# Second half of a fused vision tower: Gram products as one block, half-array routed sums, and the next rows turned ahead of the first pair's values

## The chip, the cores and the metric

The kernel runs on one core of one Trainium2 chip. The metric is the device time of one execution, in microseconds. A core has TensorE (PE in the profile; matrix products and transposes into PSUM), VectorE (DVE), ScalarE (ACT), GpSimd (POOL) and SyncE (SP, which issues the DMAs). Each engine works through its own queue in order and waits on semaphores for the others.

## What is computed

64 images of 64 patches each, 256 features, two layers of attention and feed-forward. In short:

```python
h  = patches(x) @ tokW + b                       # 64 images x 64 rows x 256
h += top-k sparse attention(layernorm(h))        # 16 heads
h += shared FFN(layernorm(h)); the routed experts' rows (2 of 8, grouped by counts)
h += polymax attention(layernorm(h)) @ W_proj
# polymax(s) = (s*s + 1 if s > 0, 1 - 0.01*s if -100 <= s <= 0, else 0) / 1000, causal
g  = gelu(rmsnorm(layernorm(h)) @ sign(w_up)-like ternary.T)
h += (g / (rms(g) + 1e-8)) @ ternary(w_down).T
```

The rms of g over its 1024 features is needed only as a factor of each output row, so the kernel multiplies first and scales afterwards.

## The kernel before

The images are taken in 8 slots of 8 images, 512 rows, four tiles of 128 rows. The first half runs the first layer's attention and shared FFN over the slots; the second half (from about 425 us) runs the second layer, slot after slot, in `slot_B(g, prev, nxt, routed)`, written out once for every engine. Slot 0 has no slot before it, slots 1 to 4 are a hardware loop (`Fori(1, LAST - 2)`, with `routed="batch"`), slot 5 is `"last"`, slot 6 has nothing routed, slot 7 has no next slot. PSUM has eight banks of 128 x 512 f32.

In slot g TensorE does, in this order: scores of tiles 2 and 3 of g; the rest of the Gram products of slot g-1; `B2_values(g, 0)`; `B3_down(g-1)` for tiles 0 and 1; the first projection; `B3_down(g-1)` for tiles 2 and 3; transposes of the next slot's normed rows `xn1` (two chunks, banks 4 and 5); `routed_sums` and `routed_turn`; `B1_qk(g+1)`; `B2_values(g, 1)`; the second projection; `routed_gates` or `routed_out`; `B1_v(g+1)`; transposes of `xn2`; scores of tiles 0 and 1 of g+1; and `B3_up(g)`.

- `B3_up` (L677) makes the eight up products (1024 hidden features, 128 at a time) into three banks. ScalarE turns each into a Gelu (L971), makes a 16-bit high half (L961), VectorE makes the low half (L1612, `g_parts`, semaphore `gl_out`).
- `gram` (L689) makes, per slice f of 128 hidden features, 16 small products whose diagonals add up to the sum of squares of each row of g. Slices 0 to 3 stand among the up products (`GRAM_LAG = 4`), slices 4 to 7 in the next slot. VectorE reads the diagonals in `mean_squares` (L1619), POOL takes the root, VectorE the reciprocal (`one_over_rms`).
- The scores become polymax weights in this way: ScalarE makes the relu (`relus`, L947) and the linear part (`lins`, L952), the square is made by VectorE for tiles 0, 1 (`v_quads`, L1562) and by ScalarE for 2, 3 (L957), VectorE adds and masks in `poly` (L1550, L1556).
- `stats3`, POOL's power (L1041) and `norm3` (L1168) norm the next slot's rows; TensorE turns them (L326); ScalarE and VectorE make 16-bit halves (L920, L1540) for `B1_qk` (L336) and `B1_v` (L621).
- `turned` (L1566) brings the values' output to SBUF for the projection (L664); `projected` (L1573) adds it to the rows; `stats4`, POOL (L1074) and `norm4` norm them for the up products; `ffn_out` (L1634) adds the FFN's output of slot g-1.
- The routed rows come in four batches of 16 groups (RB = 16). VectorE makes `one_hots` (L1477), TensorE turns them (L571) and takes gate rows from a small table (L581), VectorE weights them (`gates_in`, L1498), ScalarE and VectorE apply silu (L915, L1505), VectorE makes `weighted_hots` (L1511), and in the next slot `routed_sums` (L560) sums the batch: `wz` (128 columns) stands in the array and 64 columns of the one-hots move. In the first slot it sums zeroed buffers. `sums_in` adds the 128 x 64 result to `racc`.

Of the kernel before, what the change touches and what calls it, by code (L numbers as in the profile page):

```python
# [54 lines left out]
def build(nc, x, tokW, tokb, wqkv, bqk, bv, rW1, rb1, rW2, rb2, gateW, eb, w1, w3, w2, s1, s3, s2,  # L55
          wat, wpr, wup, wdn, ident, par, sel, delta, rev64, cmask, ridx, iota64, rev8, out):
    with ExitStack() as ctx:
# [93 lines left out]
        racc = sb("racc", [P, 64]); gT = sb("gT", [P, 64])  # L151
        UP_BANKS = (4, 7, 5)
        GRAM_LAG = 4
# [62 lines left out]
        gl_out, gT_ok, h1_mm, h1_out, h2_ok, quadv_ok = sems("gl_out gT_ok h1_mm h1_out h2_ok quadv_ok")  # L216
        h3_ok, h4_ok, h5_ok, high_w, hs_ok, hs_split, k_mm = sems("h3_ok h4_ok h5_ok high_w hs_ok hs_split k_mm")
        k_out, keep_ok, lg_ok, lin_ok, loaded_A, loaded_B = sems("k_out keep_ok lg_ok lin_ok loaded_A loaded_B")
        hs_high = sem("hs_high")
# [82 lines left out]
        def _(pe):  # L302
# [251 lines left out]
            def routed_sums(g):  # L554

                i = g - 1
# [17 lines left out]
            def routed_gates(g):  # L574

                i = g - 1
                pe.wait_ge(racc_ok, i + 2)
                pe.wait_ge(ohT_ok, i + 1)
# [8 lines left out]
            def routed_out():  # L587

                pe.wait_ge(gT_ok, 1)
                for e in range(NX):  # L590
                    m = pe.matmul(PS[0:NX, 1, 0:E], gT[:, e * NX:(e + 1) * NX], w2_s[:, e, :],
                                  start=(e == 0), stop=(e == NX - 1))
                m.then_inc(r8_mm, 1)


            def B1_qk(g, before):
# [3 lines left out]
                for c in range(C):  # L600
                    proj_T(4 + c, wat_h, E + c * P, (x1_hi, x1_lo), Bk_mm)
# [24 lines left out]
            def B2_scores(g, t):  # L626
# [4 lines left out]
                elif t == 2:  # L631
                    pe.wait_ge(lin_ok, TILES * g + 2)
# [35 lines left out]
            def B3_up(g, nxt):  # L668
                pe.wait_ge(x4T_a, 2 * g + 2)
                pe.wait_ge(x4T_v, 2 * g + 2)  # L670
                for f in range(NF):
# [8 lines left out]
                    if f >= GRAM_LAG:  # L680
                        gram(g, f - GRAM_LAG)

# [23 lines left out]
            def B3_down_last(g):  # L706

                for f in range(NF):
                    pe.wait_ge(gl_out, NF * g + f + 1)
                    if f >= NF - GRAM_LAG:  # L710
                        gram(g, f)
# [7 lines left out]
            def slot_B(g, prev, nxt, routed=None):  # L719
# [20 lines left out]
                if nxt:  # L740
                    transpose_chunk(g + 1, 0, xn1, 4, xn3_ok, x3T_mm)
                    pe.wait_ge(h4_ok, 2 * g + 1)
                    transpose_chunk(g + 1, 1, xn1, 5, xn3_ok, x3T_mm)
                if routed:
                    routed_sums(g)
                if routed == "batch":
                    routed_turn(g)
                if nxt:
                    B1_qk(g + 1, prev)
                    pe.wait_ge(Bk_out, 2 * g + 4)  # L750
                B2_values(g, 1, 4)
                B2_proj(g, 1, 4)
                if routed == "batch":
# [3 lines left out]
                if nxt:  # L757
                    B1_v(g + 1, range(TILES))
# [4 lines left out]
                if nxt:  # L763
                    if routed == "batch":
# [16 lines left out]
            attend_second(LAST, lambda c: transpose_chunk(0, c, xn1, 4 + c, xn3_ok, x3T_mm))  # L781
            pe.wait_ge(setup_b, 3)
# [11 lines left out]
            with pe.Fori(1, LAST - 2) as i:  # L794
# [8 lines left out]
        def _(act):  # L803
# [113 lines left out]
            def a_B1_x(g):  # L917
                for c in range(C):
                    act.wait_ge(x3T_mm, 2 * g + c + 1)
                    act.activation(x1_hi[:, c, 0:TOK], PS[:, 4 + c, :], ACT.Copy).then_inc(x3T_a, 1)  # L920
# [42 lines left out]
            def a_B3(g, nxt):  # L963
                if nxt:
                    relus(g + 1, 0)
                    relus(g + 1, 1)
                for f in range(NF):
# [4 lines left out]
                    if f < 2 and nxt:  # L972
                        lins(g + 1, f)
# [4 lines left out]
            def slot_B(g, prev, nxt, routed=None):  # L978
# [6 lines left out]
                if routed == "batch":  # L985
# [6 lines left out]
                if routed == "batch":  # L992
# [4 lines left out]
                if routed == "batch":  # L997
# [29 lines left out]
            lins(0, 1)  # L1027
            routed_tables()
            slot_B(0, False, True)
            with act.Fori(1, LAST - 2) as i:  # L1030
# [7 lines left out]
        def _(pool):  # L1038
# [49 lines left out]
            pool.wait_ge(cnt_ok, 1)  # L1088
            for buf in (wz, tz):
                pool.memset(buf, 0.0).then_inc(routed_zero, 1)  # L1090
            slot_B(0, False, True)
            with pool.Fori(1, LAST - 2) as i:
# [8 lines left out]
        def _(dve):  # L1101
# [37 lines left out]
            def setup_B():  # L1139

                dve.tensor_copy(identb[:, :], ident_s[:, :]).then_inc(setup_b, 1)
                dve.tensor_copy(identh[:, :], ident_s[:, :]).then_inc(setup_b, 1)
                dve.tensor_copy(cmaskb[:, :, :], cmask_s[:, :, :]).then_inc(setup_b, 1)
# [308 lines left out]
            def row_codes():  # L1452
# [18 lines left out]
                dve.wait_ge(routed_zero, 3)  # L1471
                dve.memset(racc[:, :], 0.0).then_inc(racc_ok, 1)
                dve.memset(cmp[:, 0:1], 0.0).then_inc(weighted_ok, 1)
# [331 lines left out]
```

## Time and profile before

| | us |
|---|---|
| median of 3 runs | 854.9 |
| lowest, highest | 853.94, 862.19 |
| profiled execution, its own time | 853.78 |
| span of the profiled execution | 851.9 |
| mean granted clock of TensorE, share of 2.4 GHz | 0.948 |
| TensorE, VectorE, ScalarE, GpSimd busy | 729.3, 637.6, 416.6, 83.5 |
| slot 1, slots 2 to 4, slot 5, slot 6, slot 7 (between the starts of their up products) | 51.2, 49.6, 49.6, 46.0, 42.8 |

An engine's busy time says how much work it has, not whether the end waits for it. The timeline lists groups of equal instructions in order of time; in brackets stands how long the engine had nothing to do before the group, and who released it. Where PE's rows follow each other with no bracket, PE is what the time hangs on there; where a bracket names another engine, that engine's queue is to be read.

### The profile page before, as it was taken

How to read it: one execution, taken by the hardware profiler on the slowest of the kernel's cores; microseconds unless marked ns; L12 is line 12 of the kernel's file. 1: busy time of each engine (PE TensorE's matmuls, PEld its weight loads, DVE VectorE, ACT ScalarE, POOL GpSimd, SP SyncE). 2: the span in 40 equal slices, each digit the busy share in tenths (PEclk: the TensorE clock that was granted, in tenths of full speed). 3: DMA queues.
4: the chain of work that ended last, by engine and by line, in shares of the span. 5: the costliest groups of instructions: out<-in, count | busy, mean ns of one | idle time of the engine just before them, and what ended most of it. 6: DMA issues, size and time to landing. Idle time of an engine off the chain costs nothing.

```text
span 851.9 us, 24964 instructions
## 1 busy us (share of the span) xinstructions
PE 729.3 (86%) x10597; PEld 516.7 (61%) x10597; DVE 637.6 (75%) x1437; ACT 416.6 (49%) x614; POOL 83.5 (10%) x70
## 2 busy tenths in 40 slices
PE   2869999999999999975794879898998989888857
PEld 1546676767675757653383557486775757565634
DVE  5478878787878888677599386896969688495743
ACT  4255455454646363542233382846548284554603
POOL 0001111020202020100002010010101001010000
PEclk9989999999999999995975999999999999999969
DMA  8051201020201000200000000000000000000000
GB/s 313 17 193 54 76 0 74 0 74 0 74 0 62 12 0 2 100 2 1 1 2 1 2 3 26 2 25 0 0 25 0 25 0 26 3 2 27 2 25 26
DMA packets 6790, 27.13 MB, mean 32 GB/s; under 512 B 2257, under 2 KB 3153, under 8 KB 5073
## 3 DMA queue, kind: packets, MB, share of 16 engines
q1 hardware_dynamic: 6736, 26.35, 8.3%
q8 instruction: 42, 0.69, 0.3%
q14 instruction: 12, 0.09, 0.0%
HBM read 22.15 MB, written 4.19 MB: 31 GB/s over the span
## 4 chain that ended last, share of the span: by engine, by line
PE 57%; DVE 23%; issue 10%; ACT 8%; DMA 1%; POOL 1%; DVEq 0%; SPq 0%; POOLq 0%; ACTq 0%
PE PS L336 11%; PE PS L308 7%; PE PS L347 5%; PE PS L701 5%; PE PS L440 4%; PE PS L429 3%; PE PS L664 3%; PE PS L326 3%; DVE mx L1247 3%; PE PS L641 3%; DVE Pm L1253 2%; PE PS L382 2%; PE PS L397 2%; PE PS L560 2%; DVE work L1612 2%
## 5 line engine op out<-in xcount | busy, mean ns | idle before, releaser
L308 PE MATMUL PS<-tokW_h,w_s 128*128 128x256 f16 x576 | 70.6, 282 | 18.2 <-DVE w_s L1326 18.2
L308 PEld LDWEIGHTS PS<-tokW_h,w_s 128*128 128x128 f16 x576 | 57.5, 101 | 27.2 <-issue 18.6
L848 ACT ACTIVATE PT<-PS 128x512 f32<-128x512 f32 x64 | 36.7, 596 | 76.1 <-PE PS L429 76.1
L677 PE MATMUL PS<-xT,wqkv_h 128*128 128x512 f16 x256 | 64.8, 391 | 5.4 <-ACT w_s L971 3.9
L841 ACT ACTIVATE Pm<-Pm 128x1024 f32<-128x1024 f32 x32 | 33.5, 1056 | 49.4 <-DVE Pm L1253 49.4
L336 PE MATMUL PS<-xT,wat_h 128*128 128x512 f16 x192 | 47.7, 410 | 8.4 <-DVE xT L1540 8.4
L701 PE MATMUL PS<-tokW_h,work 128*128 128x256 f16 x448 | 51.3, 273 | 0.0
L326 PE MATMUL PS<-ident_s,xn 128*128 128x128 f32 x256 | 41.2, 289 | 10.8 <-DVE xn L1168 9.7
L1247 DVE TENSOR_REDUCE mx<-PS 128x16 f32<-128x1024 f32 x32 | 39.0, 1218 | 13.1 <-PE PS L397 13.1
L1156 DVE BATCH_NORM_STATS2 st<-H 128x6 f32 (+1 forms) x128 | 46.3, 413 | 2.5
L429 PE MATMUL PS<-ident_s,Pm 128*128 128x128 f32 x256 | 40.9, 296 | 8.4 <-DVE Pm L1253 8.1
L701 PEld LDWEIGHTS PS<-tokW_h,work 128*128 128x128 f16 x448 | 43.2, 98 | 6.6 <-issue 0.2
L1612 DVE TENSOR_TENSOR work<-w_s,work 128x512 f16<-128x512 f32 x48 | 31.8, 687 | 20.3 <-ACT work L961 20.3
L664 PE MATMUL PS<-wpr_s,xT 128*128 128x256 f32 x128 | 34.6, 418 | 11.2 <-DVE xT L1566 11.2
L440 PE MATMUL PS<-vbuf,PT 128*64 128x34 f32 x1024 | 40.7, 230 | 3.6 <-ACT PT L848 3.5
L1168 DVE TENSOR_SCALAR xn<-H,mv,rstd 128x256 f32 (+1 forms) x96 | 33.8, 408 | 12.8 <-POOL rstd L1041 10.1
L440 PEld LDWEIGHTS PS<-vbuf,PT 128*64 128x64 f32 x1024 | 35.1, 142 | 13.4 <-ACT PT L848 7.9
L1041 POOL TENSOR_TENSOR rstd<-ve,mhalf 128x4 f32<-128x4 f32 x16 | 20.0, 1248 | 234.8 <-DVE ve L1164 234.8
L677 PEld LDWEIGHTS PS<-xT,wqkv_h 128*128 128x128 f16 x256 | 21.8, 100 | 34.9 <-ACT w_s L971 10.3
L937 ACT ACTIVATE vbuf<-PS 64x512 f32<-64x512 f32 x32 | 18.9, 590 | 48.5 <-PE PS L621 48.1
L1253 DVE TENSOR_TENSOR Pm<-PS,mx 128x1024 f32<-128x1024 f32 x32 | 39.2, 1224 | 3.4
L326 PEld LDWEIGHTS PS<-ident_s,xn 128*128 128x128 f32 x256 | 29.7, 145 | 18.1 <-DVE xn L1168 10.2
(240 smaller groups left out, 1629.1 us busy)
## 6 DMA issues: line engine op xcount, KB each, us to landing
work<-in_x SPq DMA_DIRECT2D x8, 1536.0 KB, 6.6
out<-H SPq DMA_DIRECT2D x8, 512.0 KB, 2.6
w_s<-in_w SPq DMA_DIRECT2D x3, 1024.0 KB, 7.4
wup_s<-in_wup SPq DMA_DIRECT2D x1, 1024.0 KB, 5.0
wdn_s<-in_wdn SPq DMA_DIRECT2D x1, 1024.0 KB, 6.9
w_s<-in_tokW SPq DMA_DIRECT2D x1, 768.0 KB, 7.5
wup_s<-in_wqkv SPq DMA_DIRECT2D x1, 768.0 KB, 8.4
wdn_s<-in_s SPq DMA_DIRECT2D x3, 256.0 KB, 6.3
```

Of the source, the lines that this page charges most:

```text
L308: m = pe.matmul(dst, halves_[xi][:, k, rows], w[:, wi, k, cols], start=(n == 0), stop=(n == 3 * chunks - 1))
L326: m = pe.transpose(PS[:, bank, t * P:(t + 1) * P], xn[:, t, c * P:(c + 1) * P], ident_s[:, :])
L336: m = pe.matmul(PS[0:cols, bank, :], w[:, wi, c, col:col + cols], x[xi][:, c, 0:TOK], start=(n == 0), stop=(n == 3 * C - 1))
L429: m = pe.transpose(PS[:, TURN_BANKS[t][half], hp * P:(hp + 1) * P], Pm[:, t % 2, at:at + P], ident_s[:, :])
L440: m = pe.matmul(PS[b * L:(b + 1) * L, 6 + t % 2, hp * 2 * VW:(hp + 1) * 2 * VW], PT[:, t % 2, hp, b * L:(b + 1) * L], Vb[:, 2 * t + b, hp, ...
L664: m = pe.matmul(PS[:, bank, (t % 2) * E:(t % 2 + 1) * E], xT2[:, c, t * P:(t + 1) * P], wpr_s[:, c, :], start=(c == 0), stop=(c == C - 1))
L677: m = pe.matmul(PS[:, UP_BANKS[f % 3], :], wup_h[:, c, f * P:(f + 1) * P], part[:, c, :], start=(k == 0), stop=(k == 2 * C - 1))
L701: m = pe.matmul(PS[:, 7 - t // 2, (t % 2) * E:(t % 2 + 1) * E], part[:, f, t * P:(t + 1) * P], wdn_h[:, f, :], start=(k == 0), stop=(k == ...
L1156: dve.bn_stats(st_[:, t, :], H[:, TILES * g + t, :]).then_inc(in_st, 1)
L1247: dve.tensor_reduce(mx[:, t % 2, :].rearrange("p (i h) -> p i h", i=4), PS[:, 0:4, hb:hb + 256].rearrange("p i (h k) -> p i h k", k=L), AX ...
L1253: dve.tensor_tensor(Pm[:, t % 2, :].rearrange("p (i h k) -> p i h k", i=4, k=L), PS[:, 0:4, hb:hb + 256].rearrange("p i (h k) -> p i h k", ...
L1612: dve.tensor_tensor(G_lo[:, f, :], g32[f], G_hi[:, f, :], ALU.subtract)\
```

## The change

- **Gram block.** `gram` is taken out of `B3_up`; all eight slices of slot g-1 stand behind the scores of tiles 2, 3 of slot g. In the last slot each slice stands ahead of its down product.
- **Order of TensorE in a slot.** Behind the Gram block come down products 0 and 1, then the transposes of the next slot's rows (now in banks 2 and 3, once the linear part of tile 3 is read), then values 0, projection, down products 2 and 3, `routed_turn`, `B1_qk`, `routed_sums`, values 1, `B1_v` of tile 0, second projection, gates, the rest of `B1_v`.
- **Routed sums.** The weighted one-hots (64 columns) stand and `wz` (128 columns) moves; even and odd groups go to the two halves of the array's columns, and `racc` holds both halves, added at the end by a product with `fold`. The sums are made a slot later, so slot 1 has none, and the zeroing of buffers for it goes. Slot 1 is written out (`routed="first"`), the loop runs from 2.
- **VectorE's order.** `norm3` stands ahead of `turned(g, 0)`, the low halves of the next rows right behind it; `weighted_hots` moves into the next slot, `one_hots` behind the first `projected`; `one_over_rms` and `ffn_out` ahead of `poly(g, 2)`; `v_B1` ahead of `stats4(g, 0)`.
- **ScalarE.** `relus(g+1, 1)` stands behind the first Gelu; the linear part of tile 1 goes to VectorE (`v_lin`), so `lin_ok` counts three per slot.

```diff
@@ routed_sums
-                pe.wait_ge(lin_ok, TILES * g + TILES)
-                pe.wait_ge(weighted_ok, i + 1)
+                pe.wait_ge(lin_ok, 3 * g + 3)
+                pe.wait_ge(weighted_ok, g - 1)
                 for k in range(RB):
-                    m = pe.matmul(PS[:, 2, 0:64], wz_k[:, k, :], one_hot_w[:, k, :],
-                                  start=(k == 0), stop=(k == RB - 1))
+                    half = slice(64 * (k % 2), 64 * (k % 2) + 64)
+                    m = pe.matmul(PS[half, 2, 0:HID], one_hot_w[:, k, :], wz_k[:, k, :],
+                                  start=(k < 2), stop=(k >= RB - 2))
@@ B3_up
-                    if f >= GRAM_LAG:
-                        gram(g, f - GRAM_LAG)
@@ TensorE slot_B
                 if prev:
                     pe.wait_ge(g_ok, NF * g)
-                    for f in range(NF - GRAM_LAG, NF):
+                    for f in range(NF):
                         gram(g - 1, f)
+                    B3_down(g - 1, (0, 1))
...
+                if nxt:
+                    pe.wait_ge(lin_ok, 3 * g + 3)
+                    for c in range(C):
+                        transpose_chunk(g + 1, c, xn1, X3_BANKS[c], xn3_ok, x3T_mm)
                 B2_values(g, 0, 4)
-                if prev:
-                    B3_down(g - 1, (0, 1))
                 B2_proj(g, 0, 5)
                 if prev:
                     B3_down(g - 1, (2, 3))
-                if nxt:
-                    transpose_chunk(g + 1, 0, xn1, 4, xn3_ok, x3T_mm)
-                    pe.wait_ge(h4_ok, 2 * g + 1)
-                    transpose_chunk(g + 1, 1, xn1, 5, xn3_ok, x3T_mm)
-                if routed:
+                if routed in ("first", "batch"):
+                    routed_turn(g)
+                if nxt:
+                    B1_qk(g + 1, prev)
+                if routed in ("batch", "last"):
                     routed_sums(g)
-                if routed == "batch":
-                    routed_turn(g)
-                if nxt:
-                    B1_qk(g + 1, prev)
+                if nxt:
                     pe.wait_ge(Bk_out, 2 * g + 4)
                 B2_values(g, 1, 4)
+                if nxt:
+                    B1_v(g + 1, (0,))
                 B2_proj(g, 1, 4)
@@ ScalarE a_B3
                     relus(g + 1, 0)
-                    relus(g + 1, 1)
                 for f in range(NF):
...
-                    if f < 2 and nxt:
-                        lins(g + 1, f)
+                    if f == 0 and nxt:
+                        relus(g + 1, 1)
+                        lins(g + 1, 0)
@@ VectorE
+            def v_lin(g):
+                if not first(g):
+                    dve.wait_ge(f2_ok, TILES * g)
+                dve.wait_ge(lin_ok, 3 * g + 1)
+                dve.tensor_scalar(lin[1][:, :].rearrange("p (i n) -> p i n", i=4), PS[:, 0:4, 256:512], 0.0, -0.01,
+                                  ALU.min, ALU.mult).then_inc(linv_ok, 1)
```

VectorE's order in a slot is then: stats3, mean_squares, norm3, turned(g, 0), v_x3T, weighted_hots, projected(g, 0), one_hots, one_over_rms, ffn_out(g - 1), poly(g, 2), poly(g, 3), v_B1, stats4(g, 0), turned(g, 1), sums_in, norm4(g, 0), projected(g, 1), stats4(g, 1), gated_sums (slot 5), first gates_in, norm4(g, 1), second gates_in, v_x4T, silus, both v_quads, v_lin, g_parts 0 to 3, poly(g + 1, 0), g_parts 4 to 7, poly(g + 1, 1).

## Rows read from the trace of the kernel before

**Rows 1.** The page: busy time of each engine, and the chain that ended last.
```profile
PE 729.3 (86%) x10597; PEld 516.7 (61%) x10597; DVE 637.6 (75%) x1437; ACT 416.6 (49%) x614; POOL 83.5 (10%) x70
PE 57%; DVE 23%; issue 10%; ACT 8%; DMA 1%; POOL 1%; DVEq 0%; SPq 0%; POOLq 0%; ACTq 0%
```

**Rows 2.** Busy time in windows, one per slot: slots 1, 2, 5, 6, 7.
```profile
488.38:539.57 51.19, 45.56 (x732) 33.04 (x729) 39.06 (x85) 30.04 (x42) 4.99 (x4) 1.00 0.03 12
...
589.18:638.79 49.61, 45.17 (x732) 33.15 (x729) 40.95 (x87) 28.64 (x41) 4.99 (x4) 1.00 0.03 11
...
688.43:738.00 49.57, 45.44 (x700) 31.74 (x696) 36.63 (x84) 24.66 (x38) 4.17 (x4) 1.00 0.03 12
738.00:784.00 46.00, 38.96 (x653) 26.82 (x649) 33.84 (x79) 24.67 (x38) 4.17 (x4) 1.00 0.04 13
784.00:826.80 42.80, 29.30 (x452) 20.05 (x449) 28.63 (x62) 18.98 (x28) 3.02 (x3) 0.85 0.04 14
```

**Rows 3.** Timeline, start and duration in us: the up products of slot 2.
```profile
591.20 0.60 ACT L971 ACTIVATE w_s<-PS 128x512 f32<-128x512 f32 x1
591.67 1.04 ACT L952 ACTIVATE u<-PS 128x1024 f32<-128x1024 f32 x1
...
593.96 0.68 ACT L961 ACTIVATE work<-w_s 128x512 f16<-128x512 f32 x1
...
599.50 0.30 PE L689 MATMUL PS<-work 128*32 128x64 f16 x16 [1.61 <-DVE work L1612]
...
601.19 0.61 PE L635 MATMUL PS<-cmaskb,identb 128*128 128x256 bf16 x4 [0.19 <-issue]
601.21 1.22 DVE L1556 SCALAR_TENSOR_TENSOR Pm<-late,hs 128x1024 f32<-128x1024 f32 x1
```

**Rows 4.** Timeline, from the scores to the sums (last row: POOL in slot 5).
```profile
604.37 0.83 PE L689 MATMUL PS<-work 128*32 128x64 f16 x64
604.76 1.40 DVE L1156 BATCH_NORM_STATS2 st<-H 128x6 f32 x4
605.06 1.10 PE L655 MATMUL PS<-Pm,vbuf 128*32 128x64 f32 x64
606.10 3.67 PE L701 MATMUL PS<-tokW_h,work 128*128 128x256 f16 x32
606.73 1.97 POOL L1041 TENSOR_TENSOR rstd<-ve,mhalf 128x4 f32<-128x4 f32 x1 [23.49 <-DVE ve L1164]
609.60 1.89 PE L664 MATMUL PS<-wpr_s,xT 128*128 128x256 f32 x8
615.70 3.68 PE L560 MATMUL PS<-wdn_s,wup_s 128*128 128x64 f32 x32
...
705.99 1.01 POOL L1041 TENSOR_TENSOR rstd<-ve,mhalf 128x4 f32<-128x4 f32 x1 [23.49 <-DVE ve L1164]
```

**Rows 5.** Timeline, from the key products to the next up products.
```profile
570.71 5.35 PE L336 MATMUL PS<-xT,wat_h 128*128 128x512 f16 x24
572.22 1.41 DVE L1534 TENSOR_SCALAR kM<-PS,par_s 128x512 f32<-128x512 f32 x2
577.91 1.99 PE L664 MATMUL PS<-wpr_s,xT 128*128 128x256 f32 x8 [0.81 <-DVE xT L1566]
584.07 0.74 DVE L1168 TENSOR_SCALAR xn<-H,mv,r 128x256 f32 x2
```

**Rows 6.** Timeline: 64 standing columns in alternate halves, f16, then f32.
```profile
631.33 2.87 PE L621 MATMUL PS<-wat_h,xT 128*64 128x128 f16 x96
...
202.49 1.13 PE L440 MATMUL PS<-vbuf,PT 128*64 128x34 f32 x32
```

**Rows 7.** Timeline behind two long waits of PE, and a window of slot 0.
```profile
468.51 7.40 PE L336 MATMUL PS<-xT,wat_h 128*128 128x512 f16 x24 [4.24 <-DVE xT L1540]
...
815.36 3.78 PE L664 MATMUL PS<-wpr_s,xT 128*128 128x256 f32 x8 [4.69 <-DVE xT L1566]
...
456.00:462.00 6.00, 4.69 (x71) 3.94 (x72) 5.42 (x19) 3.61 (x4) 1.01 (x1) 0.50 0.02 3
```

More of the change, by code:

```diff
@@ L150, in build @@
         PH = PS[:, 0:2, :].rearrange("p b n -> p (b n)").bitcast(F16)
[L151 removed]
+        racc = sb("racc", [P, HID]); fold = sb("fold", [P, 64]); gT = sb("gT", [P, 64])
         UP_BANKS = (4, 7, 5)
[L153 removed]
+        X3_BANKS = (2, 3)
+        FIRST_BANKS = (4, 3)
         TURN_BANKS = ((4, 5), (4, 5), (0, 1), (2, 3))
@@ L587, in routed_out @@
             def routed_out():
+                pe.wait_ge(racc_ok, LAST - 2)
+                pe.matmul(PS[:, 0, 0:64], racc[:, :], fold[:, :], start=True, stop=True).then_inc(gT_mm, 1)
                 pe.wait_ge(gT_ok, 1)
@@ L600, in B1_qk @@
                 for c in range(C):
+                    if not first(g) and c == 1:
+                        pe.wait_ge(h4_ok, 2 * g - 1)
                     proj_T(4 + c, wat_h, E + c * P, (x1_hi, x1_lo), Bk_mm)
@@ L757, in slot_B @@
                 if nxt:
-                    B1_v(g + 1, range(TILES))
+                    B1_v(g + 1, range(1, TILES))
                     pe.wait_ge(Bv_out, 4 * g + 6)
@@ L763, in slot_B @@
                 if nxt:
-                    if routed == "batch":
+                    if routed in ("first", "batch"):
                         pe.wait_ge(wz_ok, 2 * g)
@@ L793, in _ @@
             slot_B(0, False, True)
-            with pe.Fori(1, LAST - 2) as i:
+            slot_B(1, True, True, routed="first")
+            with pe.Fori(2, LAST - 2) as i:
                 slot_B(i, True, True, routed="batch")
@@ L919, in a_B1_x @@
                     act.wait_ge(x3T_mm, 2 * g + c + 1)
-                    act.activation(x1_hi[:, c, 0:TOK], PS[:, 4 + c, :], ACT.Copy).then_inc(x3T_a, 1)
+                    bank = (FIRST_BANKS if first(g) else X3_BANKS)[c]
+                    act.activation(x1_hi[:, c, 0:TOK], PS[:, bank, :], ACT.Copy).then_inc(x3T_a, 1)
             def a_B1_k(g):
@@ L984, in slot_B @@
                     a_B1_x(g + 1)
-                if routed == "batch":
+                if routed in ("first", "batch"):
                     one_hot_turned(g)
@@ L991, in slot_B @@
                     a_B1_v(g + 1, 0)
-                if routed == "batch":
+                if routed in ("first", "batch"):
                     routed_tanh(g, 0)
@@ L996, in slot_B @@
                     a_B1_v(g + 1, 1)
-                if routed == "batch":
+                if routed in ("first", "batch"):
                     routed_tanh(g, 1)
@@ L1026, in _ @@
             lins(0, 0)
-            lins(0, 1)
             routed_tables()
             slot_B(0, False, True)
-            with act.Fori(1, LAST - 2) as i:
+            slot_B(1, True, True, routed="first")
+            with act.Fori(2, LAST - 2) as i:
                 slot_B(i, True, True, routed="batch")
@@ L1086, in slot_B @@
                 p_ln4(g, 1)
-            pool.wait_ge(cnt_ok, 1)
-            for buf in (wz, tz):
-                pool.memset(buf, 0.0).then_inc(routed_zero, 1)
             slot_B(0, False, True)
-            with pool.Fori(1, LAST - 2) as i:
+            slot_B(1, True, True, routed="first")
+            with pool.Fori(2, LAST - 2) as i:
                 slot_B(i, True, True, routed="batch")
@@ L1142, in setup_B @@
                 dve.tensor_copy(identh[:, :], ident_s[:, :]).then_inc(setup_b, 1)
+                dve.tensor_tensor(fold[:, :], ident_s[:, 0:64], ident_s[:, 64:P], ALU.add).then_inc(setup_b, 1)
                 dve.tensor_copy(cmaskb[:, :, :], cmask_s[:, :, :]).then_inc(setup_b, 1)
@@ L1677, in slot_B @@
                 v_x4T(g)
-                if routed == "batch":
+                if routed in ("first", "batch"):
                     silus(g)
-                    weighted_hots(g)
                 if nxt:
@@ L1719, in first_polys @@
                 v_quads(0, 1)
+                v_lin(0)
                 poly(0, 0)
@@ L1727, in _ @@
             slot_B(0, False, True)
-            with dve.Fori(1, LAST - 2) as i:
+            slot_B(1, True, True, routed="first")
+            with dve.Fori(2, LAST - 2) as i:
                 slot_B(i, True, True, routed="batch")
```

96 lines of the change are left out of this document (50 added, 46 removed).

## The prediction

> **What bounds the kernel now.** I read the page first: TensorE is busy 86% of the span, VectorE 75%, ScalarE 49% [rows 1]. All of the change but three small edits lies in the second half, so I then cut that half into slots, from the first up product of one slot to that of the next [rows 2]. Slots 2 to 4 take 49.6 us each (slot 1, with a table load of ScalarE and a longer wait at its start, 51.2), slot 5 49.6, slot 6 46.0, slot 7 42.8. In a looped slot PE is busy 45.2 of 49.6 us: mostly a PE-bound slot, and its few idle stretches tell what else bounds it.
>
> The timeline of one looped slot (T is 589.18, where its up products start) shows three stretches. First the up products [rows 3]: 8 products of about 0.9 us would be 7.1 us, but they last until 601.19, 12.0 us. ScalarE holds them: it does two relus before the first Gelu at T+2.02 and two linear parts among the Gelus, and PE waits for VectorE's low halves before a Gram product (idle 1.61 ahead of one of them). Then a stretch that PE fills without idling: scores, Gram remainder, values 0, down products, projection, next rows' transposes, weighted sums [rows 4]. Last the part with short waits of PE, from the query and key products to the next up products [rows 5]. Values 0 start at T+15.88, and from there to the next T are 33.73 us.
>
> **The change, part by part, in a looped slot.** I walk both orders from the same T, with durations and start-to-start distances of rows 3 to 5.
>
> *Up products.* ScalarE: relu 0 starts at T+0.2 and takes 0.92 to its successor; the first Gelu then starts at T+1.1 instead of T+2.02; relu 1 T+1.6, linear part T+2.5, second Gelu T+3.4, first high half T+3.9, and from there one Gelu and one high half per 1.0 us [rows 3], so high half 3 ends at T+7.6 and high half 7 at T+11.1 (it ended at T+13.26 before). PE, free of Gram products here and ahead by the earlier Gelus, ends its ups at T+8.0 and the two scores (1.59 each) at T+11.2, against T+15.2 before. So PE gains 4 us here.
>
> *VectorE in the same stretch.* It loses weighted_hots (1.22, moved) and gets v_lin. The trace has no such instruction; the nearest are the 128x1024 ones at 1.22 us, 1.14 to the next start; between 1.0 (ScalarE's own [rows 3]) and 1.41 (two 128x512 scalings out of PSUM [rows 5]) I take 1.14. Squares at T+1.2 and T+2.6, v_lin T+3.8, low halves 0 to 3 paced by the high halves until T+8.2, poly 0 2.5 us to T+10.7, low halves 4 to 7 (0.6 each) to T+13.1, poly 1 2.4 us to T+15.5, stats3 1.9 to T+17.4. Before, VectorE was at stats3 at T+15.58: it comes 0.1 us earlier, not 4. The Gelus' gain is eaten by v_lin and by VectorE's own queue.
>
> *The Gram block* waits for the last low half, T+13.1, and is done at T+13.4. In a block 64 products take 0.69 us, one slice of 16 alone 0.23 plus 0.07 more for the up product behind it [rows 3, 4], so the block costs about as much as it saves (0.7 more here, 1.2 less among the ups).
>
> *Next rows ahead.* Down products 0 and 1 (3.5) run from T+13.4 to T+16.9. The transposes then wait for norm3: stats3 at T+17.4, POOL's power 1.01 (it took 1.97 while one_hots ran beside it, 1.01 in slot 5, which has none [rows 4]; one_hots is moved away), the four normalizations 1.4: last row at T+19.9. The third linear part, also awaited, is there at T+18.6. PE idles 2.7 of the 3.5 us from T+16.9, and values 0 start at T+20.4. Before they started at T+15.9 with less behind them: 3.5 us of down products and 0.9 of transposes are now done. The first stretch has thus gained nothing (20.4 against 15.9 + 4.4 = 20.3).
>
> *From values 0 to the next T.* The 33.73 lose the down products (3.50), transposes (0.88), most of the 0.81 wait ahead of the second projection (B1_v of tile 0, 0.71, now covers it), and part of the sums. They gain a 0.88 wait ahead of the first projection (values, then VectorE's xT, then PE, which the down products had covered; the same chain cost 0.81 [rows 5]). And as only three value tiles (2.1 us for 2.84) stand between the second projection and the x4 transposes, the chain projection, stats4, POOL 1.01, norm4, gate scaling (together 4.9 us from 579.90 to xn2's last row at 584.81 [rows 5]) shows with 0.5 us of wait. Sums aside: 33.73 - 3.50 - 0.88 - 0.64 + 0.88 + 0.5 = 30.1.
>
> *Half-array sums.* Now 32 instructions take 3.61 us, 113 ns each, though 64 columns move. Turned round, 64 columns stand and 128 move, in alternate halves. The nearest rows: f16, same shape, halves in turn, 2.87 us for 96, 30 ns; f32 with 64 standing columns, halves in turn, 33 ns with 34 moving [rows 6]. An f32 instruction with 256 moving columns takes 216 ns [rows 4], so 128 take about 108, in two halves 54: 32 x 54 = 1.7 us. Lower end 1.5 (what the 33 ns leave beyond their columns is shared too), upper end 3.5 (halves don't overlap). I take 1.7, as the f32 row with halves shows overlap: 34 columns alone would be 29 ns, loads come on top and still 33 is seen. That saves 1.9: 30.1 - 1.9 = 28.2.
>
> A rule against it: the Trainium skill (TensorEngine Tiling (Array Packing), Key Properties) says that changing the tiling mode drains the array. The change adds about three such changes in a slot (sums, value tile 0 split off) and takes out eight around the Gram slices. By the rows a Gram slice among ups costs 0.14 more than one in a block, both changes of mode in it; by that the rule is in the walk already, and at 0.07 per change the three are worth 0.2 us per slot. The trace agrees that a change costs something; it isn't in my sum.
>
> In all, a looped slot: 20.4 + 28.2 = 48.6, plus 0.2 for register waits in the loop (a polynomial in the loop starts its halves 1.34 apart, in the unrolled slots 1.25): 48.8 against 49.6, **-0.8**. The three remaining looped slots: -2.4.
>
> **Slots 1, 5, 6, 7 and 0.** Slot 1, unrolled, has no sums: 1.7 less, but then values 1 wait for v_B1, which VectorE now does behind ffn_out and both polynomials: PE's query and key products end about 0.9 us before. 48.6 - 1.7 + 0.9 = 47.8, for 49.6 before (the 1.6 of 51.2 that its start costs stays on either side): **-1.7**. Slot 5: no turn and gates (-1.0, -1.9), but routed_out (3.6) now waits for fold, gated_sums, which stand behind the second projection's add and stats4 on VectorE, 2.1 us; 48.6 - 2.9 + 3.6 + 0.3 (fold) + 2.1 - 0.9 (waits that these cover) = 50.8 against 49.6: **+1.1**. Slot 6 has nothing routed, so what was 46.0 is only exposed: 48.6 - 1.7 - 2.9 = 44.0, plus 1.9 wait for v_B1 and 1.8 more for norm4 - 0.5 = 47.2: **+1.2**. It also lost no sums to save. Slot 7: polynomials 2 and 3 stand behind ffn_out, values 1 wait 5.4 us for them in two parts; before, the second projection waited 4.69 for the same queue [rows 7]. Down products moved earlier make up for it: **+0.2**. Slot 0: v_lin (1.1) lengthens VectorE's chain before values 0, but the early x3 halves take away the 4.24 us wait ahead of the key products [rows 7], while values and projection come later: **-0.4**, between -2 and +1.5, since PE runs there at 1.2 GHz (clock 0.50 before 462 us) either way. The last slot's ups, Gram and down products are the same work in another order: 0. At the setup, fold's 0.1.
>
> **Sum:** -2.4 - 1.7 + 1.1 + 1.2 + 0.2 - 0.4 + 0.1 = -1.9. The profiled execution took 853.8 (span 851.9): 851.9. The median of the three runs shown is 854.9, 1.1 above it, and I take that on: **853.0 us**.
>
> **Rivals.**
> *Halves don't overlap* (sums stay at 3.5): for it, the f32 rows with halves move only 34 columns and are load-heavy. 1.8 x 4 slots = +7.2: 860.
> *The clock falls.* PE runs at full clock in all slots 1 to 6 now. New is a stretch of 3.5 us ahead of values 0 in which PE works 0.8. Twice in the trace a stretch without work was followed by 1.2 GHz: 4.24 us ahead of 468.51, where 24 key and query instructions then took 7.40 instead of 5.35, and 4.69 ahead of 815.36, where a projection took 3.78 instead of 1.89 [rows 5, 7]. Against it: the idle 1.61 in the ups [rows 3] left the clock of its slot at 1.00 [rows 2]. If it falls in each of six slots, values and projection cost 0.9 + 1.8 more: 6 x 2.7 = +16, 869; four slots decide for slower. The Trainium skill (TensorE: Matmul & The Clock Gate, Part 1: The HAM clock gate) has an idle array go to 1.2 GHz; by that rule this rival would be the outcome if the transposes come later than I have them.
> *Many small waits.* Each mode change and each register wait is a little longer than I have it, v_lin at 1.4, v_B1 late in the looped slots too: +0.9 in six slots, 858.
> *VectorE hides it.* Were norm3's rows there when the down products end, 2.7 us of idle in each of six slots would go: 853 - 16 = 837. It needs VectorE to reach stats3 2.7 us earlier; the queue [rows 3] speaks against it, unless poly 1 or v_lin is much cheaper.
>
> **Chances.** Forecast 0.64, halves 0.10, small waits 0.10, clock 0.08, hidden 0.08. About 1% (8.5 us) is what a measurement of this kernel can tell from no change. Halves and small waits stay within it. Faster by over 1%: 0.10 (hidden, and some of my own error); slower: 0.10; within: 0.80. The range 847 to 861 leaves out clock and hidden, 0.16, and a little more.
>
> **What would show it.** The first Gelu 1.1 us behind the first up product; scores done at T+11.2; PE idle ahead of the x3 transposes about 2.7 us, ended by norm3; the sums at 1.7 us; looped slots 48.8, slots 5 and 6 longer than before. I am wrong if the idle ahead of the transposes is under 1 us, if the sums stay over 3 us, or if the granted clock leaves 1.0 in slots 1 to 6.

## The result: 1.7% slower, and the profile after

The changed kernel took 871.6 us (median of four, 867.5 to 872.7) against 855.1 before (median of four, 853.9 to 862.2); the ratio is 1.017, with an interval of 1.010 to 1.023. It is slower, by 1 to 2%. The profiled execution spans 868.8 us, before 851.9: 16.9 us more. I had forecast 2 us less.

The slots first, since the forecast was made by slots. Here is busy time in windows of the changed kernel, one for each of the slots 1 to 7. The window of slot g begins where the up products of slot g-1 begin, at T, and ends where those of slot g begin; the column behind POOL is the granted clock as a share of full speed. Before, the windows of slots 2 to 4 were 49.6 us each, all at 1.00 ([rows 2]; by this count its row from 589.18 on is slot 3, though it is called slot 2 there).

```profile
491.73:541.25 49.52, 44.01 (x701) 29.89 (x697) 40.74 (x85) 29.14 (x41) 4.16 (x4) 0.98 0.03 12
541.25:593.53 52.28, 48.02 (x732) 33.34 (x728) 42.52 (x88) 27.75 (x40) 4.17 (x4) 0.93 0.03 12
593.53:644.27 50.74, 46.41 (x732) 32.62 (x728) 42.42 (x88) 27.86 (x40) 4.16 (x4) 0.97 0.03 11
644.27:694.81 50.54, 46.22 (x732) 32.38 (x728) 42.43 (x88) 27.86 (x40) 4.16 (x4) 0.97 0.03 10
694.81:750.50 55.69, 49.68 (x702) 32.90 (x699) 38.03 (x85) 23.76 (x37) 4.16 (x4) 0.91 0.03 11
750.50:799.46 48.96, 41.24 (x652) 28.24 (x648) 35.63 (x80) 23.88 (x37) 4.16 (x4) 0.97 0.03 13
799.46:842.95 43.49, 29.99 (x453) 20.68 (x450) 29.99 (x63) 18.08 (x27) 3.03 (x3) 0.87 0.04 13
```

| | before | forecast | after |
|---|---|---|---|
| up to slot 0's up products | 488.4 | 488.1 | 491.7 |
| slot 1 | 51.2 | 49.5 | 49.5 |
| slots 2, 3, 4 | 49.6 each | 48.8 each | 52.3, 50.7, 50.5 |
| slot 5 | 49.6 | 50.7 | 55.7 |
| slot 6 | 46.0 | 47.2 | 49.0 |
| slot 7 | 42.8 | 43.0 | 43.5 |

Slot 1 is as forecast. In every slot from 2 to 6, where the clock was 1.00 before, it is now 0.91 to 0.97, and each of them is longer than the walk by 1.7 to 5 us.

Where it falls shows in the timeline of TensorE in slot 3, with T = 593.53 (before: [rows 3, 4]):

```profile
593.53 3.63 PE L682 MATMUL PS<-xT,wqkv_h 128*128 128x512 f16 x16
597.62 4.04 PE L682 MATMUL PS<-xT,wqkv_h 128*128 128x512 f16 x16 [0.46 <-ACT w_s L976]
...
604.67 1.19 PE L692 MATMUL PS<-work 128*32 128x64 f16 x96
606.16 0.30 PE L692 MATMUL PS<-work 128*32 128x64 f16 x16 [0.30 <-DVE work L1626]
606.76 0.30 PE L692 MATMUL PS<-work 128*32 128x64 f16 x16 [0.30 <-DVE work L1626]
607.00 3.67 PE L704 MATMUL PS<-tokW_h,work 128*128 128x256 f16 x32
612.50 2.30 PE L327 MATMUL PS<-ident_s,xn 128*128 128x128 f32 x8 [1.83 <-DVE xn L1173]
614.72 1.94 PE L660 MATMUL PS<-Pm,vbuf 128*32 128x64 f32 x64
617.47 1.99 PE L669 MATMUL PS<-wpr_s,xT 128*128 128x256 f32 x8 [0.81 <-DVE xT L1580]
```

The up products end at T+8 and PE sits idle 1.83 us ahead of the transposes, ended by VectorE's norm3: both as in the walk. Then the transposes take 2.30 and values 0 take 1.94 us instead of 1.10: PE is at the lower of its two levels, 1.2 GHz. Here are windows of the same stretch:

```profile
606.00:610.00 4.00, 3.54 (x60) 3.06 (x61) 3.97 (x7) 2.70 (x3) 0.00 (x0) 1.00 0.00 0
610.00:614.00 4.00, 2.17 (x13) 1.30 (x11) 2.87 (x19) 2.15 (x4) 2.14 (x2) 0.91 0.00 0
614.00:618.00 4.00, 3.19 (x70) 2.58 (x69) 1.27 (x3) 1.17 (x2) 0.00 (x0) 0.67 0.00 0
618.00:622.00 4.00, 4.00 (x32) 3.47 (x31) 3.74 (x7) 0.00 (x0) 0.00 (x0) 1.00 0.00 0
```

The lower clock comes behind the emptiest stretch of the slot and ends once PE is filled again. Slot 5 has it twice, the second time behind 2.15 us idle ahead of `routed_out`, whose 16 instructions then take 5.31 us (3.62 before). In slots 2 and 5 it also lasts longer than in slot 3: there the projection takes 3.78 us instead of 1.99 too. The queue of VectorE is where I had it (timeline, slot 3):

```profile
597.33 1.22 DVE L1575 TENSOR_SCALAR late<-PS 128x1024 f32<-128x1024 f32 x1
...
607.88 1.22 DVE L1563 SCALAR_TENSOR_TENSOR Pm<-late,hs 128x1024 f32<-128x1024 f32 x1
609.02 1.40 DVE L1161 BATCH_NORM_STATS2 st<-H 128x6 f32 x4
...
612.03 1.38 DVE L1173 TENSOR_SCALAR xn<-H,mv,rstd 128x256 f32 x4 [0.51 <-POOL rstd L1047]
```

v_lin (L1575) takes 1.22 and stats3 starts at T+15.5, where the walk had it. So VectorE reaches norm3 no earlier than before, and what PE gains in the up products it loses in one stretch, waiting for norm3.

### The profile page after: what moved, and what is told of

It is laid out like the page before. It is cut to its first block, busy times and chain, and to the rows that moved or that the text cites. A ratio compares the mean times of both kernels' runs of the same rounds, so it can differ in the third digit from the quotient of the medians.

```text
span 868.8 us, 24871 instructions
## 1 busy us (share of the span) xinstructions
PE 743.6 (86%) x10567; PEld 519.1 (60%) x10567; DVE 649.2 (75%) x1444; ACT 409.9 (47%) x606; POOL 76.7 (9%) x68
## 4 chain that ended last, share of the span: by engine, by line
PE 48%; issue 22%; DVE 20%; ACT 6%; POOL 2%; DMA 1%; DVEq 0%; POOLq 0%; SPq 0%; ACTq 0%
PE PS L337 8%; PE PS L309 7%; PE PS L348 5%; PE PS L441 4%; PE PS L430 3%; PE PS L669 3%; PE PS L327 3%; PE PS L704 2%; DVE mx L1252 2%; DVE Pm L1258 2%; PE PS L383 2%; PE PS L398 2%; PE PS L416 2%; PE PS L660 2%; PE PS L646 1%
## 5 line engine op out<-in xcount | busy, mean ns | idle before, releaser
L327 PE MATMUL PS<-ident_s,xn 128*128 128x128 f32 x256 | 48.8, 308 | 30.2 <-DVE xn L1173 23.1
L327 PEld LDWEIGHTS PS<-ident_s,xn 128*128 128x128 f32 x256 | 31.5, 150 | 43.3 <-DVE xn L1173 22.9
L846 ACT ACTIVATE Pm<-Pm 128x1024 f32<-128x1024 f32 x32 | 33.6, 1058 | 48.8 <-DVE Pm L1258 48.8
L337 PE MATMUL PS<-xT,wat_h 128*128 128x512 f16 x192 | 45.8, 398 | 2.5 <-DVE xT L1544 2.5
L669 PE MATMUL PS<-wpr_s,xT 128*128 128x256 f32 x128 | 39.1, 458 | 7.4 <-DVE xT L1580 7.3
L441 PEld LDWEIGHTS PS<-vbuf,PT 128*64 128x64 f32 x1024 | 36.1, 145 | 13.4 <-ACT PT L853 7.8
L1047 POOL TENSOR_TENSOR rstd<-ve,mhalf 128x4 f32<-128x4 f32 x16 | 16.1, 1007 | 289.0 <-DVE ve L1169 289.0
```

Of the source, the lines that this page charges most:

```text
L327: m = pe.transpose(PS[:, bank, t * P:(t + 1) * P], xn[:, t, c * P:(c + 1) * P], ident_s[:, :])
L337: m = pe.matmul(PS[0:cols, bank, :], w[:, wi, c, col:col + cols], x[xi][:, c, 0:TOK], start=(n == 0), stop=(n == 3 * C - 1))
L441: m = pe.matmul(PS[b * L:(b + 1) * L, 6 + t % 2, hp * 2 * VW:(hp + 1) * 2 * VW], PT[:, t % 2, hp, b * L:(b + 1) * L], Vb[:, 2 * t + b, hp, ...
L669: m = pe.matmul(PS[:, bank, (t % 2) * E:(t % 2 + 1) * E], xT2[:, c, t * P:(t + 1) * P], wpr_s[:, c, :], start=(c == 0), stop=(c == C - 1))
```

## The experiments

Two theories stood against each other. *Clock*: the new stretch of idle and sparse work on PE lets the clock fall, and the lower clock costs the time. *Work and waits*: the parts of the change cost more than the walk says, and the clock is a by-stander.

### Filling the idle stretch: e1, e9, and a control e10

```diff
                     B3_down(g - 1, (0, 1))
+                    if nxt:
+                        for k in range(16):
+                            pe.matmul(PS[:, 5, 0:E], G_hi[:, k % NF, 0:P], wdn_h[:, k % NF, :], start=True, stop=True)
```

> The changed kernel with 16 products of 128x256 f16 that nobody reads added on PE between down products 0, 1 and the transposes of the next rows (slots 1 to 6), about 1.75 us in a stretch where PE is idle 1.83 to 1.93 us. Clock theory (the idle stretch lets the clock fall, and the lower clock stretches what follows): the granted clock stays at 1.00 behind that place in slots 2, 3, 4 and 6 and for one of two drops in slot 5; slots 2, 3, 4, 5, 6 lose 3.4, 1.7, 1.7, 3.4, 1.7 us, the whole about 12: 859 to 861. Rival (the time is lost in the waits themselves, the clock follows from something else): the waits move as before, nothing is gained or up to 1 us per slot is lost: 871 to 876.

Measured: 865.3 us (ratio to before 1.010, 1.005 to 1.015), 6.3 below the changed kernel. Timeline of slot 3, T = 592.28, with the 16 products at L733 (e9 has 8 of them):

```profile
609.24 1.91 PE L733 MATMUL PS<-tokW_h,work 128*128 128x256 f16 x16
611.24 1.73 PE L327 MATMUL PS<-ident_s,xn 128*128 128x128 f32 x8
612.90 1.10 PE L660 MATMUL PS<-Pm,vbuf 128*32 128x64 f32 x64
```

The transposes start at T+19.0, as in the changed kernel: they come no earlier. But values 0 take 1.10 again, and the slot 49.3 us instead of 50.7; the difference of 1.4 is what transposes and values 0 lost to the clock (0.57 and 0.84). The total came out 4 to 6 us above what I had expected. Slot 2, 51.6 us, has a fall at another place: its down products take 5.18 for 3.67, behind 1.39 us within a Gram slice in which PE waits for nothing that the profile shows ("issue"). It stands in slot 2, the first of the loop, in the other runs of this order too (0.32 us in the changed kernel, 1.17 in e9, 1.42 in e10); why its length varies is left open. Slot 5 kept the fall at `routed_out`, and slot 6 got a new one behind its 2.00 us wait for norm4: 50.7 us.

> As e1_fill16 with 8 instead of 16 products that nobody reads (0.9 us of the 1.9 us of idle). If how much work the stretch holds decides: the falls that e1_fill16 took away in slots 2 to 4 stay in some of them, 866 to 871, or go (then 865).

Measured: 861.5 us (ratio 1.004, 1.000 to 1.007), below both of the outcomes that I had named. Half the filling did at least as well. Windows of slots 2 to 5:

```profile
540.70:590.10 49.40, 45.66 (x740) 32.16 (x736) 42.38 (x88) 27.75 (x40) 4.16 (x4) 1.00 0.03 13
590.10:639.50 49.40, 45.97 (x741) 32.26 (x738) 42.48 (x88) 27.75 (x40) 4.16 (x4) 1.00 0.03 11
...
688.80:740.00 51.20, 46.04 (x711) 31.38 (x708) 37.92 (x85) 23.76 (x37) 4.16 (x4) 1.00 0.03 12
```

In these slots this is the changed kernel at full clock: looped slots of 49.3 to 49.4, a quarter of a microsecond below before, where I had 0.8. Two falls are left in e9, in slot 0's scores and in slot 6 (50.7 us, behind the wait for norm4 as in e1).

> Control for e1_fill16: the same 16 products that nobody reads, behind down products 2 and 3, where PE is never idle. Clock theory: the falls stay as in the changed kernel, since the stretch ahead of the transposes is as empty as before, and 1.75 us per slot come on top in slots 1 to 6: about 881 (878 to 884). If any extra work anywhere holds the clock: 866 to 876.

```diff
                     B3_down(g - 1, (2, 3))
+                if prev and nxt:
+                    pe.wait_ge(h4_ok, 2 * g + 1)
+                    for k in range(16):
+                        pe.matmul(PS[:, 5, 0:E], G_hi[:, k % NF, 0:P], wdn_h[:, k % NF, :], start=True, stop=True)
```

Measured: 873.6 us (ratio 1.019, 1.012 to 1.025), below my 878 to 884 and inside the 866 to 876 that I had named for extra work holding the clock wherever it stands. The profiled execution is the fastest of the four (868.7; the others 872.8 to 875.2, at a lower mean clock), so the others may have had more falls than it shows. Slots 2 to 4:

```profile
538.30:589.40 51.10, 46.84 (x748) 33.04 (x744) 42.33 (x88) 27.73 (x40) 4.15 (x4) 1.00 0.03 13
589.40:641.90 52.50, 48.19 (x749) 34.19 (x746) 42.47 (x88) 27.84 (x40) 4.16 (x4) 0.97 0.02 10
641.90:692.90 51.00, 46.70 (x748) 33.02 (x744) 42.33 (x88) 27.73 (x40) 4.16 (x4) 1.00 0.03 10
```

Slots 3 and 4 have the same 1.83 us wait ahead of their transposes, but only slot 3 has the fall:

```profile
608.39 2.25 PE L327 MATMUL PS<-ident_s,xn 128*128 128x128 f32 x8 [1.83 <-DVE xn L1177]
610.57 1.94 PE L660 MATMUL PS<-Pm,vbuf 128*32 128x64 f32 x64
...
660.81 1.73 PE L327 MATMUL PS<-ident_s,xn 128*128 128x128 f32 x8 [1.83 <-DVE xn L1177]
662.48 1.10 PE L660 MATMUL PS<-Pm,vbuf 128*32 128x64 f32 x64
```

(In slot 2 the wait is 0.23 us, and 1.42 us of issue stand within a Gram slice.) So my control didn't keep the falls, and it can't say by its total that the place of the filling matters; what filling that stretch does is shown by e5 below, against e2. It says something else: one and the same stretch may bring the fall or not. Slot 1 of the changed kernel says so too: it has the same wait, 1.93 us, and its values 0 take 1.10 (its 0.98 is from the beginning of the slot, left over from slot 0). In the slots without a fall the length is 49.4 plus 1.7, the added products, which fits both theories; slot 3's extra 1.4 fits the clock alone.

### The Gram block alone, and filled: e2, e5

```diff
-        GRAM_LAG = 4
+        GRAM_LAG = NF
...
-                    for f in range(NF - GRAM_LAG, NF):
+                    for f in range(NF):
                         gram(g - 1, f)
```

> The kernel before with one part alone: all Gram slices as one block behind the scores of tiles 2 and 3. The walk gives values 0 about 1 us earlier per slot (the block waits for the last low half, which comes slightly earlier): about 850 (847 to 856). If the block is what lowers the clock (few columns, waits of PE before it), the clock falls in slots 1 to 6 and it takes over 860.

Measured: 863.8 us (ratio 1.009, 1.007 to 1.012): my walk of it, 850, was wrong, and the clock fell in slots 1 to 6, as the last sentence has it. A window and the timeline of slot 3 (T = 594.97):

```profile
594.97:646.20 51.23, 46.77 (x733) 34.20 (x729) 41.10 (x87) 28.54 (x41) 4.99 (x4) 0.97 0.02 10
...
607.02 0.73 PE L689 MATMUL PS<-work 128*32 128x64 f16 x64
608.89 0.30 PE L689 MATMUL PS<-work 128*32 128x64 f16 x16 [1.14 <-DVE work L1611]
...
610.69 0.30 PE L689 MATMUL PS<-work 128*32 128x64 f16 x16 [0.30 <-DVE work L1611]
610.86 1.65 PE L655 MATMUL PS<-Pm,vbuf 128*32 128x64 f32 x64
612.44 4.73 PE L701 MATMUL PS<-tokW_h,work 128*128 128x256 f16 x32
```

Values 0 start at T+15.89, exactly as before (T+15.88): the block gains nothing, as VectorE's low halves set its end. Behind the block, which ends in small products with waits of 1.14 and three of 0.30 between them, values take 1.65 for 1.10 and down products 4.73 for 3.67. Slots 2 to 5 are 51.2 us each for 49.6, and slots 1 and 6 are 1.6 longer too.

e5 adds this to it:

```diff
                     for f in range(NF):
+                        if f == 4:
+                            for k in range(10):
+                                pe.matmul(PS[:, 5, 0:E], G_hi[:, k % 4, 0:P], wdn_h[:, k % 4, :], start=True, stop=True)
                         gram(g - 1, f)
```

> The kernel before with the Gram block alone, as in e2_gram_block, and 10 products of 128x256 f16 that nobody reads put ahead of the block's slice 4, where PE is idle 1.14 us. Clock theory: in e2_gram_block each slot has one fall of 3.4 us of granted clock behind the block, which costs 1.6 us; with the stretch filled the clock stays at 1.00 in slots 2 to 5, a slot takes 49.5 instead of 51.2 us, the whole 853 to 857. Rival (the block itself costs 1.6 us per slot, whatever the clock): 862 to 866.

Measured: 855.3 us (ratio 0.999, 0.997 to 1.002). In slot 3 (T = 589.50, filling at L728):

```profile
589.50:639.10 49.60, 46.30 (x742) 34.12 (x738) 40.95 (x87) 28.55 (x41) 4.99 (x4) 1.00 0.03 11
...
602.24 1.26 PE L728 MATMUL PS<-tokW_h,work 128*128 128x256 f16 x10
603.43 0.30 PE L689 MATMUL PS<-work 128*32 128x64 f16 x16
...
605.39 1.10 PE L655 MATMUL PS<-Pm,vbuf 128*32 128x64 f32 x64
606.42 3.67 PE L701 MATMUL PS<-tokW_h,work 128*128 128x256 f16 x32
```

Values 0 start at T+15.89 here too, and 1.2 us of useless work makes the kernel 8.4 us faster than without it. The edit does nothing else. This shows the clock as the cause of what the block costs: the same work ends at the same times up to values 0, and a slot takes 49.6 us with the stretch filled and 51.2 with it open.

### Undoing the Gram block in the changed kernel: e6

```diff
                     m.then_inc(up_mm, 1)
+                    if f >= 4:
+                        gram(g, f - 4)
...
-                    for f in range(NF):
+                    for f in range(4, NF):
                         gram(g - 1, f)
```

> The changed kernel with one part undone: Gram slices 0 to 3 are back among the up products, slices 4 to 7 behind the scores. PE's waits for VectorE are then spread over the ups again and the wait ahead of the transposes shrinks from 1.9 us to about 0.5, while VectorE's chain to norm3, which sets the start of values 0, is the same. Clock theory: granted clock 1.00 in slots 1 to 4, slots of 49.3, the whole about 857 (854 to 861). Rival (the early transposes alone keep the clock falling): over 866.

Measured: 871.5 us (ratio 1.020, 1.017 to 1.022), the same as the changed kernel: the rival's number. Timeline of slot 3 (T = 593.26):

```profile
612.51 2.01 PE L327 MATMUL PS<-ident_s,xn 128*128 128x128 f32 x8 [1.88 <-DVE xn L1176]
614.45 1.94 PE L660 MATMUL PS<-Pm,vbuf 128*32 128x64 f32 x64
```

The wait ahead of the transposes is still 1.88 us; I had it at 0.5, as I had taken the ups' end from before, while ScalarE's earlier Gelus end them at T+10 even with the Gram slices among them. So undoing the block removes none of the wait, and none of the falls: slots 1 to 5 have the same clocks (0.98, 0.93, 0.97, 0.97, 0.91) and, within 0.1 us, the same lengths as in the changed kernel. The block alone can bring the fall (e2), but in the changed kernel the early transposes are enough.

### One part alone: the half-array sums, e3

> The kernel before with one part alone: the routed sums turned round and in half-array pairs, still five of them and in their old place. 1.7 us less in each of five slots if PE's queue is what counts there: 846.5 (844 to 850). If it is hidden behind the halves of the next rows (x3) that the key products wait for: 850 to 855.

```diff
-                    m = pe.matmul(PS[:, 2, 0:64], wz_k[:, k, :], one_hot_w[:, k, :],
-                                  start=(k == 0), stop=(k == RB - 1))
+                    half = slice(64 * (k % 2), 64 * (k % 2) + 64)
+                    m = pe.matmul(PS[half, 2, 0:HID], one_hot_w[:, k, :], wz_k[:, k, :],
+                                  start=(k < 2), stop=(k >= RB - 2))
...
```

(The edit also has the product by `fold` in slot 5, and `v_B1` there ahead of `gated_sums`.)

Measured: 851.0 us (ratio 0.993, 0.990 to 0.997), just outside the 844 to 850 that I had expected; but the gain is not hidden. Slots 2 to 4 take 48.1 each, 1.5 less; the first of them:

```profile
540.50:588.50 48.00, 43.48 (x732) 31.24 (x728) 40.62 (x87) 28.65 (x41) 4.99 (x4) 1.00 0.03 11
```

Two places gave part of it back. Slot 0's scores of tile 1 ran at 1.2 GHz (the first up product at 490.2 instead of 488.4), though the transposes ahead of them start at 484.3 in both kernels. And slot 6 took 46.4 for 46.0.

### Removing the wait: e4, e7, e8

The walk says what keeps PE waiting: norm3 comes behind poly 1 and stats3 on VectorE. e4 gives PE other work until then. The cut below is PE's part of the edit; the order of VectorE is changed too, as the expectation has it, and ScalarE makes the key and query parts ahead of the turned one-hots.

```diff
                     B3_down(g - 1, (0, 1))
...
+                B2_values(g, 0, 4)
+                if prev:
+                    B3_down(g - 1, (2, 3))
                 if nxt:
                     pe.wait_ge(lin_ok, 3 * g + 3)
                     for c in range(C):
                         transpose_chunk(g + 1, c, xn1, X3_BANKS[c], xn3_ok, x3T_mm)
-                B2_values(g, 0, 4)
                 B2_proj(g, 0, 5)
-                if prev:
-                    B3_down(g - 1, (2, 3))
-                if routed in ("first", "batch"):
-                    routed_turn(g)
                 if nxt:
                     B1_qk(g + 1, prev)
+                if routed in ("first", "batch"):
+                    routed_turn(g)
```

> The changed kernel with PE's order Gram block, down products 0 and 1, values 0, down products 2 and 3, transposes of the next rows, projection, key and query products, one-hots turned, sums; VectorE in the matching order (mean squares, stats3, turned, norm3, poly 2, low halves of x3, projected, ffn_out, weighted hots, one hots, poly 3). Nothing then waits for norm3. Clock theory: no stretch of idle PE ahead of the transposes, clock 1.00 in slots 1 to 6, a looped slot about 45.7 us: 830 to 842. Rival (the clock falls through the Gram block and its waits): still over 855.

Measured: 835.8 us (ratio 0.977, 0.972 to 0.982): 36 us below the changed kernel, with the same products in another order. A looped slot takes 47.0 us (I had 45.7). The clock is the smaller part of that gain: slots 2 to 4 take 51.2 us on average in the changed kernel, 49.4 in e9 at full clock, and 47.0 here, so that 1.8 us of a slot are the falls and 2.4 the wait and what else the order saves.

> e4_later_turn with the product by fold ahead of slot 5's second projection and gated_sums ahead of VectorE's second projected: the 2.15 us wait ahead of routed_out goes. Slot 5 takes 46 instead of 48 us: 833.5 to 834.5. If the wait only moves to another place: no difference to 835.8.

Measured: 829.4 us (ratio 0.971, 0.968 to 0.973), 6.3 less where I expected 2. Slots 5, 6 and 7 of e7:

```profile
674.40:720.40 46.00, 44.22 (x702) 30.16 (x698) 37.91 (x85) 23.77 (x37) 4.17 (x4) 1.00 0.04 13
720.40:763.70 43.30, 39.06 (x652) 26.93 (x648) 35.59 (x80) 23.76 (x37) 4.17 (x4) 1.00 0.04 14
763.70:802.70 39.00, 28.70 (x453) 19.75 (x450) 29.72 (x63) 18.08 (x27) 3.03 (x3) 0.91 0.04 15
```

Slot 5 lost the 2 us of the wait (48.0 to 46.0). Another 4.5 are slots 6 and 7 (46.4 to 43.3, 40.3 to 39.0): in e4 slot 6's scores and ups ran at 1.2 GHz behind its wait for norm4, in e7 the same wait, ended half a microsecond earlier in time (759.63 for 760.15), brought no fall.

> e7_early_fold with products that nobody reads in PE's idle stretches of slots 6 and 7 (16 ahead of slot 6's x4 transposes; 30, 38 and 10 ahead of slot 7's second projection, x4 transposes and up products). Clock theory: slot 6's scores and ups and slot 7's projection and ups run at full clock: 1.9 + 1.7 + 1.9 + 1.9 us less, 826 to 829. If work nobody reads doesn't hold the clock: 834 or more.

Measured: 826.5 us (ratio 0.966, 0.963 to 0.969), as expected by the clock theory, but only 3.0 below e7, since e7 had already lost slot 6's fall (the filling there changes nothing, 43.3 us with and without it) and slot 7 was 1.4 shorter. The filling in slot 7 did what it was to do; timeline, with the filling at L772 and L776:

```profile
794.25 4.31 PE L772 MATMUL PS<-tokW_h,work 128*128 128x256 f16 x38
...
799.86 1.25 PE L776 MATMUL PS<-tokW_h,work 128*128 128x256 f16 x10
801.69 7.07 PE L680 MATMUL PS<-xT,wqkv_h 128*128 128x512 f16 x32 [0.57 <-DVE xT L1629]
```

The 32 up products take 7.07 us; in e7, behind 4.10 and 1.50 us of idle, they took 8.72 (9.93 in the changed kernel).

## Why the prediction was wrong

- **The step that failed is the clock rival.** I wrote that against it stood "the idle 1.61 in the ups [rows 3] left the clock of its slot at 1.00", gave it 0.08, left it out of the sum and let the range stop at 861. The clock fell in slots 2 to 6, to 0.91 to 0.97 of the slot, which was one of my signs of being wrong. The mechanism and the place were as the rival had them: the stretch ahead of the transposes, a fall behind it, a price on what follows. That 1.61 stood between up products of full size; the new wait stands behind Gram slices with waits between them and ahead of transposes that wait row by row, with another 0.8 us of idle ahead of values 0. I had also tied the rival to transposes that come later than in the walk; they didn't, and the clock fell all the same. And the trace of before held nearer cases than 1.61 and 4.24, in its first half:

```profile
401.98 8.23 PE L336 MATMUL PS<-xT,wat_h 128*128 128x512 f16 x24 [2.47 <-DVE xT L1540]
...
422.09 2.79 PE L308 MATMUL PS<-late,th 128*128 128x256 f16 x24 [2.24 <-DVE th L1303]
```

  Behind 2.24 us the clock stayed at 1.00, but behind 2.47, which followed f32 transposes and products of 34 columns, 24 key and query products took 8.23 us for 5.35. Less idle than the forecast 2.7 us had thus been followed by a fall, and the case deserved far more than 0.08.
- **Its price** was put at 2.7 us in each of six slots. It was 1.2 to 1.4 us in slots 3, 4 and 6 (transposes and values alone), 2.9 in slot 2, where the projection ran at 1.2 GHz too, none in slot 1, and some 4.5 in slot 5, where a second fall came at a wait that I had priced at its 2.1 us alone. Together about 11.5 of the 16.9 us (slots 2 to 5 against e9, slot 6 by its rows). That the rival's total, 869, lies near the measured 871.6 is luck: its falls were too dear, and the 2.2 us and the 3 us below weren't in it.
- **Up to slot 0's up products** I had -0.3 with the setup; it was +3.3. Of this 1.2 us is there when the x4 transposes begin: 0.6 comes from the first half, and `v_lin` puts VectorE's chain 1.1 back. PE waits 6.32 us for ScalarE's last linear part ahead of the x3 transposes. The 4.24 us wait is gone, as forecast, and the key and query products run at 2.4 GHz (5.39 us for 7.40), where I had 1.2 GHz on either side; but values 1 then wait 1.70 us for `v_B1`. The other 2.2 are the next scores, which run at 1.2 GHz behind a 2.13 us wait for norm4 (from the second part of x4's transposes to the first up product 6.3 us, 4.1 before).
- **The walk at full clock** held. Slot 1: -1.7 forecast, -1.7 measured. Scores' end at T+11.1 (forecast T+11.2), last Gram slice at T+13.5 (13.4), stats3 at T+15.5 (15.5), PE's idle ahead of values 0 2.6 us in all (2.7), values 0 at T+20.6 (20.4), the last two in slots without a fall. A looped slot: 49.35 for 48.8; from values 0 to the next T 28.7 instead of 28.4. Two sums of the prediction are a tenth off, and cancel: by its own terms slot 1 is -1.8 and slot 5 +1.2.
- **The sums**, with halves: 1.97 us for 32 (1.90 to the next start), 1.7 forecast, 3.68 before. The Trainium skill (TensorEngine Tiling (Array Packing), Theoretical Speedup) has up to twice for a dimension of at most 64; the trace agrees, with 1.9 times. The exchange of the standing and the moving side is in that figure too, and no run takes the two apart.
- **Slot 5** at full clock was to be +1.1; e9, at 1.00 throughout, has 51.2, which is +1.6. **Slot 6** is 47.6 without its fall of 1.4, +1.6 for the forecast +1.2.
- **The sum.** Slots, start and tail without the falls in slots 2 to 6 and in slot 0's scores add up to about +3 us against my -1.9 (16.9 - 11.5 - 2.2). e9 gives nearly the same: its span is 7.5 us above before, of which slot 0's scores are 2.2 and slot 6's new fall 3.1. So at full clock, by this estimate, the change would have been no gain, and no loss that can be told from none. What made it a loss is that I priced waits as waits. Here an empty stretch can have a second price, paid behind it.

## What to carry to other kernels

When a reordering gathers TensorE's small waits into one stretch, look at the granted clock behind that stretch before looking at anything else, and ask of the walk not only how long PE waits but what stands around the wait. The remedy is other work for the stretch (values 0 and down products 2 and 3 ahead of the transposes: 871.6 to 835.8 us, in the looped slots the larger part of it without the clock); where there is none, a microsecond of products that nobody reads can pay for itself, as 863.8 to 855.3 shows. And a part of a change that frees an engine which then waits for the same other engine gains nothing: the Gram block moved values 0 by 0.01 us.

## What the runs showed of the hardware that I had not expected

- A wait of 1.0 to 1.2 us and three of 0.30 between slices of 16 small products (128x32 standing, 64 moving) were followed by 1.2 GHz in each of slots 1 to 6 of e2; 10 products of 128x256 in the first of these waits kept 2.4 GHz in all six (e5).
- The same wait in the same surroundings brings the fall or doesn't: 1.83 us in e10, slot 3 but not slot 4; 2.00 us at slot 6, in e4 but not in e7. Why the fall came at one and not at the other is left open; the slots differ in when the wait comes. So such a kernel's time can move by some microseconds for changes that touch nothing nearby. The kernel before does so by itself: of its 13 executions beside e5, 11 took 853.5 to 857.4 us, at mean clocks of 0.940 to 0.950, and two 861.6 and 861.7, at 0.937. No trace shows where the clock fell in those two.
- Filling less can do more: 8 products (861.5 us) against 16 (865.3), the difference lying in slots 2 and 5, where the falls came elsewhere.
- f32 products with 64 standing and 128 moving columns in alternate halves took 59 ns each, against 113 ns for 128 standing and 64 moving.
